# A two-layer attention and expert kernel: the up stage in another order, the attention's last rows in banks of their own, part of the routing on ScalarE

## The chip, the cores and the metric

One core of a Trainium2 chip runs the whole program. The time is that of the device for one execution, in microseconds (us). Before the change the median of three executions is 611.51 us.

## What is computed

The reference runs two layers over `x` (16 positions x 128 rows of 256 features, float32), each an attention and a feed-forward part with a layer norm ahead and a residual sum behind. The parts that the change touches are the first layer's quantized feed-forward part, the second layer's attention, and its routed experts.

```python
x = act_qdq(x)                                   # scale from max|x|, rounded to 16-bit steps
up = act_qdq(x @ lpbq_dequant(w_up).T)           # 256 -> 768
gate = act_qdq(x @ lpbq_dequant(w_gate).T)
gate = act_qdq(gate * fixed_qdq_u16(sigmoid(gate)))
o = act_qdq(gate * up); return o @ lpbq_dequant(w_down).T
...
scores = einsum('bhqd,bhkd->bhqk', q, k) / sqrt(16)      # 16 heads of 16, 16 batches of 128
out = einsum('bhqk,bhkd->bhqd', softmax(scores), v) @ w_o.T + b_o
...
logits = layernorm(x) @ w_router                          # 2048 tokens, 8 experts, top 2
pos = cumsum(mask_kt, axis=1) * mask_kt - 1.0             # place in the expert, capacity 160
y = combine(gate, relu(dispatch(x) @ wi) @ wo)            # expert width 1024
```

## The kernel before

Each engine has its own hand-written queue of instructions; semaphores (`s[...]`) order them against each other. There is no scheduler, so the order in the code of an engine is the order on the chip. The 16 batches are called rows here, numbered 0 to 15 (`NB` = 16). PSUM is cut into eight banks `ps[0]` to `ps[7]`; the names `pA`, `pB`, `pC` in a profile are banks 0 to 3, 4 and 5, 6 and 7.

The **up stage** begins when the gate product has been computed for all tokens and its overall maximum is known. TensorE makes 24 pieces of the up product (`product`, 128 x 512 each, bank `ps[2 + f]`). ScalarE moves each out of PSUM (`evacuate`, L632) and VectorE takes its maximum (`piece_max`, L1066). Beside that, 16 gate pieces of 128 x 768 go through five steps: to integers (`g_to_int`, on ScalarE at L646 for even pieces, on VectorE at L1091 for odd ones), sigmoid (L659, ScalarE), rounding (L664, ScalarE), product (`gate_sig`, L1095, VectorE) and maximum (`gs_max`, L1099, VectorE). The buffers `GI`, `SG` and `SI` of these steps hold two pieces each. The queues are loops over four chunks. At the end `whole_max(2, 2)` gathers the two maxima, and nothing of the next stage starts before them.

The **second attention** walks the rows with a lag: at step t, scores of row t+1, turned probabilities of row t and t-1 (`turn_0` to `turn_3`, L1652, copied out by `pt_copy`, L746), values of row t-1 (L1661), and the output of rows t-2 and t-3 (`o_turn` L1714, `attn_out` L1242, `a_turn` L1725, `a_out` L1731, `add_attn` L1228). All rows share banks 6 and 7 for turned probabilities and for `o_turn`, bank 5 for values and bank 4 for the output.

Behind the last row a layer norm (`norm4`, L868, in pairs of rows) feeds `d_turn` (L1743, copied out by `xt4`, L754) and the router's logits: rows 0 to 7 in one group (`d_logits`, L1751), rows 8 to 15 one by one (`d_row`, L1770). VectorE then finds the two best experts (one-hots in `OH`, L1322), the places, and which token fills which place of expert 0 (`select`, L1348, 16 compares of 128 x 192 in bf16). POOL reads the chosen rows with three indirect transfers (`rows_in`, L508), TensorE turns them (`e_turn`, L1868) and the first expert's products start (L1884). `keep_busy` (L1399) are TensorE products that nothing reads.

## Time and profile before

| | |
|---|---|
| median of 3 executions | 611.51 us (611.19 to 614.05) |
| the profiled execution | 611.87 us, of which its span is 610.1 us |
| TensorE matmul busy | 519.4 us (85% of the span) |
| VectorE busy | 387.2 us (63%) |
| ScalarE busy | 306.2 us (50%) |
| POOL busy | 152.6 us (25%) |

A row of the timeline gives the start, the time, the engine, the line of the kernel, the operation, output<-input, and in brackets how long the engine had been idle before it and who released it. The distance between two starts on one engine can be shorter than the duration, since an instruction without a wait starts before the one ahead has ended.

### The profile page before, as it was taken

How to read it: one execution, taken by the hardware profiler on the slowest of the kernel's cores; microseconds unless marked ns; L12 is line 12 of the kernel's file. 1: busy time of each engine (PE TensorE's matmuls, PEld its weight loads, DVE VectorE, ACT ScalarE, POOL GpSimd, SP SyncE). 2: the span in 40 equal slices, each digit the busy share in tenths (PEclk: the TensorE clock that was granted, in tenths of full speed). 3: DMA queues.
4: the chain of work that ended last, by engine and by line, in shares of the span. 5: the costliest groups of instructions: out<-in, count | busy, mean ns of one | idle time of the engine just before them, and what ended most of it. 6: DMA issues, size and time to landing. Idle time of an engine off the chain costs nothing.

```text
span 610.1 us, 9357 instructions
## 1 busy us (share of the span) xinstructions
PE 519.4 (85%) x3284; PEld 366.7 (60%) x3284; DVE 387.2 (63%) x944; ACT 306.2 (50%) x577; POOL 152.6 (25%) x218
## 2 busy tenths in 40 slices
PE   0859999799989900799989999986699999999994
PEld 0638866654434400687757677775566776777673
DVE  5666689845469989888699799986423332133101
ACT  1526658823389969781287788874022122211220
POOL 2715525000000000000323133111224445434431
PEclk9979999989989965899999999999599999999998
DMA  7900000000000000016000001015114445453410
GB/s 216 309 4 2 1 2 1 2 0 1 0 0 0 1 0 1 1 65 211 0 1 3 19 18 37 2 36 173 26 51 161 148 161 178 135 179 125 130 44 21
DMA packets 31994, 37.57 MB, mean 62 GB/s; under 512 B 8657, under 2 KB 27729, under 8 KB 31953
## 3 DMA queue, kind: packets, MB, share of 16 engines
q1 hardware_dynamic: 28880, 29.07, 14.6%
q0 software_dynamic: 3072, 7.95, 4.5%
q8 instruction: 26, 0.43, 0.3%
q14 instruction: 16, 0.12, 0.1%
HBM read 30.14 MB, written 6.88 MB: 61 GB/s over the span
## 4 chain that ended last, share of the span: by engine, by line
PE 58%; DVE 21%; ACT 11%; issue 6%; SPq 1%; DMA 1%; POOLq 0%; DVEq 0%; POOL 0%; ACTq 0%
PE pA L1884 11%; PE pB L1902 9%; PE pC L1614 6%; DVE rm L1248 5%; PE pA L1646 3%; DVE arena L1257 3%; PE pA L1576 3%; ACT arena L595 2%; PE pC L1488 2%; PE pC L1576 2%; PE pB L1576 2%; ACT XIT L684 2%; PE pC L1895 2%; ACT XIT L679 2%; DVE am L1066 1%
## 5 line engine op out<-in xcount | busy, mean ns | idle before, releaser
L474 POOL TENSOR_TENSOR arena<-KT,par 128x256 f32<-128x256 f32 x32 | 18.9, 612 | 254.2 <-DVE XIT L1171 191.5
L1884 PE MATMUL pA<-arena 128*128 128x320 f32 x256 | 74.1, 438 | 0.9 <-ACT arena L817 0.9
L824 ACT ACTIVATE arena<-pA 128x320 f32<-128x320 f32 x64 | 28.0, 437 | 71.9 <-PE pA L1884 71.2
L1902 PE MATMUL pB<-arena 128*128 128x256 f32 x256 | 59.3, 385 | 0.0
L1884 PEld LDWEIGHTS pA<-arena 128*128 128x128 f32 x256 | 47.4, 190 | 19.4 <-issue 1.1
L1902 PEld LDWEIGHTS pB<-arena 128*128 128x128 f32 x256 | 47.4, 190 | 9.4 <-issue 3.1
L1066 DVE TENSOR_REDUCE am<-arena 128x1 f32<-128x512 f32 (+1 forms) x48 | 32.0, 681 | 23.9 <-ACT arena L632 23.9
L1614 PE MATMUL pC<-wdnT,XIT 128*128 128x256 f32 x192 | 42.9, 381 | 1.8 <-DVE XIT L1171 1.8
L1614 PEld LDWEIGHTS pC<-wdnT,XIT 128*128 128x128 f32 x192 | 36.0, 190 | 7.9 <-DVE XIT L1171 2.8
L1652 PE MATMUL pC<-ident,arena 128*128 128x128 f32 x256 | 37.8, 280 | 2.7 <-DVE arena L1242 1.2
L1248 DVE TENSOR_REDUCE rm<-pA 128x16 f32<-128x2048 f32 x16 | 36.7, 2291 | 2.8 <-PE pA L1646 2.0
L1257 DVE TENSOR_TENSOR arena<-pA,rm 128x1024 f32<-128x1024 f32 x32 | 37.7, 1220 | 0.5
L746 ACT ACTIVATE arena<-pC 128x512 f32<-128x512 f32 x64 | 36.5, 594 | 2.4 <-PE pC L1652 2.2
L817 ACT ACTIVATE arena<-pA 128x320 f32<-128x320 f32 x16 | 6.1, 435 | 62.4 <-PE pA L1868 62.4
L510 POOL DMA_INDIRECT out<-arena,token x24 | 23.5, 978 | 54.8 <-DVE arena L1379 44.9
L508 POOL DMA_INDIRECT arena<-token_rows,token x24 | 24.2, 1010 | 46.8 <-DVE token L1358 27.0
L1652 PEld LDWEIGHTS pC<-ident,arena 128*128 128x128 f32 x256 | 27.9, 141 | 12.1 <-issue 8.3
L1364 DVE COPY gcol<-arena 128x3 f32<-128x3 f32 x8 | 1.4, 181 | 53.1 <-DMA arena<-token_rows,token 53.1
L735 ACT ACTIVATE arena<-arena 128x1024 f32<-128x1024 f32 x32 | 33.6, 1052 | 1.7 <-DVE arena L1257 0.7
L1399 PE MATMUL pB<-ident 128*128 128x128 f32 x66 | 12.1, 362 | 21.6 <-DVE arena L1144 21.6
L508 POOL DMA_INDIRECT arena<-out,token x24 | 23.7, 988 | 9.3 <-issue 7.0
L1399 PEld LDWEIGHTS pB<-ident 128*128 128x128 f32 x66 | 11.4, 271 | 21.7 <-issue 21.6
(316 smaller groups left out, 1134.4 us busy)
## 6 DMA issues: line engine op xcount, KB each, us to landing
arena<-in_L_ffn_wi SPq DMA_DIRECT2D x8, 1024.0 KB, 5.4
arena<-in_L_ffn_wo SPq DMA_DIRECT2D x8, 1024.0 KB
X<-in_x SPq DMA_DIRECT2D x4, 512.0 KB, 6.1
arena<-in_ctx SPq DMA_DIRECT2D x4, 512.0 KB, 5.7
out<-X SPq DMA_DIRECT2D x4, 512.0 KB, 3.0
token_rows<-arena SPq DMA_DIRECT2D x4, 512.0 KB, 5.6
arena<-in_L_ffn_w_up SPq DMA_DIRECT2D x1, 768.0 KB, 8.9
arena<-in_L_ffn_w_gate SPq DMA_DIRECT2D x1, 768.0 KB, 10.3
```

Source lines behind the costliest of these rows:

```text
L508: return nc.gpsimd.indirect_dma_start(out=sbuf[0:n, c, :], out_offset=None, in_=dram, in_offset=where, bounds_check=NB * S - 1, oob_is_err ...
L735: nc.scalar.activation(part, part, ACT.Exp).then_inc(s["p_ready"], 1)
L746: nc.scalar.activation(PT[:, u, 4 * g:4 * g + 4, :], pC[:, BANK_OF[g], :].rearrange("p (k n) -> p k n", k=4), ACT.Copy).then_inc(s["pt_rea ...
L824: nc.scalar.activation(HT[:, u, f, :], ps[2 + f % 2][:, 0:ROWS], ACT.Relu).then_inc(s["h_relu"], 1)
L1066: V_.tensor_reduce(am[:, 0 if name == "gate" else 1, cols(c * FT + f, 1)], t[:, f, cols(c, 512)], AX.X, ALU.max, apply_absolute_value=True ...
L1248: V_.tensor_reduce(rm[:, u, :], sco, AX.X, ALU.max).then_inc(s["rm_ready"], 1)
L1257: V_.tensor_tensor(PR[:, u, part], sco[:, part], rm[:, u, part].unsqueeze(2).broadcast_to([P, NH1 // 2, P]), ALU.subtract).then_inc(s["s_s ...
L1576: last = mm(ps[2 + f][:, :], w[:, k, f * P:(f + 1) * P], XITv[:, k, cols(c, 512)], start=(k == 0), stop=(k == KD - 1))
L1614: last = mm(ps[6 + u][:, 0:D], OT[:, u, f, :], wdnT[:, f, :], start=(f == 0), stop=(f == FT - 1))
L1652: last = tr(pC[:, BANK_OF[g], n * P:(n + 1) * P], PR[:, u, 4 * g + n, :], ident[:, :])
L1884: last = mm(ps[2 + f % 2][:, 0:ROWS], WI[:, u, k, f * P:(f + 1) * P], XET[:, u, k, :], start=(k == 0), stop=(k == KD - 1))
L1902: last = mm(ps[4 + c][:, 0:D], HT[:, u, f, c * P:(c + 1) * P], WO[:, u, f, :], start=(f == 0), stop=(f == NFT - 1))
```

## The change

Six edits are made together.

1. Up stage. The loops are written out. `GI` holds four pieces instead of two, and `SI` moves into the tensor `wgtT`. VectorE turns pieces 0, 1, 2, 4, 5, 8, 11 and 12 into integers (`GATE_DVE`), ScalarE the other eight. ScalarE moves up pieces 0 and 1 out ahead of the wait for the gate's scale; TensorE makes up piece 0 and half of piece 1 around the two small products of `whole_max(1, 1)`.
2. End of the second attention. Row 15's probabilities are turned into banks 0 to 3, its values go to bank 0 and its `o_turn` to bank 6; the outputs of rows 14 and 15 go to banks 3 and 5. The end of the walk is written out in a new order on three engines. The norm of rows 8 and 9 is made ahead of row 14's output, and that of rows 4 to 7 moves from VectorE to ScalarE (`norm4_act`).
3. Logits of rows 8 to 11 are made in one group of eight narrow products (`d_logits4`) and turned back (`d_back4`), in place of eight products of 8 columns.
4. The one-hots are written with the 8 rows of a group innermost, which is their order in memory. Before, the expert was innermost, at a step of 32 bytes in the output.
5. Expert 0's compares for rows 12 to 15 (`SEL_DVE` = 12) go to ScalarE, as Abs and then Relu, two instructions a row.
6. Expert 0's three transfers have a semaphore each. Each is turned when it lands, with 13, 4 and 2 `keep_busy` products ahead instead of 20, and ScalarE copies the result in two instructions, the first ahead of the last transfer's part.

Some semaphores are folded into others. The prefetch of expert weights waits for `u_again` in place of `g2_again`, one ScalarE instruction later.

```diff
+        GATE_DVE = (0, 1, 2, 4, 5, 8, 11, 12)
...
+        SEL_DVE = 12
         BANK_OF = (1, 1, 0, 0)
+        OUT_BANK = [4] * (NB - 2) + [3, 5]
...
-            g_to_int(0, 0)
-            up_chunk(0)
-            with act.Fori(1, 3) as c:
-                up_chunk(c)
-            up_chunk(3)
+            def g_to_int(b):
+                if b >= 4:
+                    act.wait_ge(s["gs_done"], b - 3)
+                nc.scalar.activation(GI[:, b % 4], F_b(G, b), ACT.Copy, scale=sc[:, 7:8]).then_inc(s["g_int_act"], 1)
+            def sigmoid(b):
+                mine = sum(r in GATE_DVE for r in range(b + 1))
+                if b in GATE_DVE:
+                    act.wait_ge(s["g_int_dve"], mine)
+                else:
+                    act.wait_ge(s["g_int_act"], b + 1 - mine)
+                if b >= 2:
+                    act.wait_ge(s["sig_int"], b - 1)
+                nc.scalar.activation(SG[:, b % 2], GI[:, b % 4], ACT.Sigmoid, scale=sc[:, 5:6]).then_inc(s["sig"], 1)
+            def sig_round(b):
+                act.wait_ge(s["sig"], b + 1)
+                if b >= 2:
+                    act.wait_ge(s["gs_done"], b - 1)
+                nc.scalar.activation(SI[:, b % 2], SG[:, b % 2], ACT.Copy, scale=65536.0).then_inc(s["sig_int"], 1)
+            def up_evacuate(lo, hi):
+                for n in range(lo, min(hi, 4 * FT)):
+                    evacuate(U, "up", n // FT, n % FT)
+            up_evacuate(0, 2)
+            for b in range(NB):
+                n = 2 + 3 * (b // 2) + b % 2
+                if b == 0:
+                    act.wait_ge(s["sc_gate"], 1)
+                sigmoid(b)
+                up_evacuate(n, n + 1)
+                sig_round(b)
+                if b % 2:
+                    up_evacuate(n + 1, n + 2)
+                if b + 2 < NB and b + 2 not in GATE_DVE:
+                    g_to_int(b + 2)
...
+            def g_to_int(b):
+                if b >= 4:
+                    dve.wait_ge(s["gs_done"], b - 3)
+                V_.tensor_scalar(GI[:, b % 4], F_b(G, b), sc[:, 7:8], None, ALU.mult).then_inc(s["g_int_dve"], 1)
+            def gate_sig(b):
                 dve.wait_ge(s["sig_int"], b + 1)
-                V_.tensor_tensor(F_b(G, b), GI[:, u], SI[:, u], ALU.mult).then_inc(s["gs_done"], 1)
+                V_.tensor_tensor(F_b(G, b), GI[:, b % 4], SI[:, b % 2], ALU.mult).then_inc(s["gs_done"], 1)
...
-            up_chunk(0)
-            with dve.Fori(1, 4) as c:
-                up_chunk(c)
+                V_.tensor_reduce(am[:, 0, cols(b, 1)], F_b(G, b), AX.XY, ALU.max, apply_absolute_value=True).then_inc(s["up_max"], 1)
+            def up_max(lo, hi):
+                for n in range(lo, min(hi, 4 * FT)):
+                    piece_max(U, "up", n // FT, n % FT)
+            g_to_int(0)
+            g_to_int(1)
+            up_max(0, 3)
+            g_to_int(2)
+            for b in range(NB):
+                n = 3 + 3 * (b // 2) + b % 2
+                gate_sig(b)
+                if b >= 1:
+                    gs_max(b - 1)
+                up_max(n, n + 1 + b % 2)
+                if b + 3 < NB and b + 3 in GATE_DVE:
+                    g_to_int(b + 3)
             gs_max(NB - 1)
...
+            u = (NB - 1) % 2
+            rsqrt(6, 12)
+            pt_copy(NB - 1, u, 0)
+            pt_copy(NB - 1, u, 1)
+            pt_copy(NB - 1, u, 2)
+            pt_copy(NB - 1, u, 3)
+            os_copy(NB - 2, 1 - u)
+            at_copy(NB - 3, u)
+            os_copy(NB - 1, u)
+            act.wait_ge(s["xr_ready"], 1)
+            norm4_act(4)
+            norm4_act(5)
+            at_copy(NB - 2, 1 - u)
+            at_copy(NB - 1, u)
+            norm4_act(6)
+            norm4_act(7)
+            xt4(0)
+            xt4(1)
...
+                if t == NB - 1:
+                    dve.wait_ge(s["row_stats"], 2 * NB + 12)
+                    variances(12, D)
                 if 0 <= t - 3 < NB:
                     add_attn(t - 3)
                 if 0 <= t - 2 < NB:
                     attn_out(t - 2, t % 2)
+            u = (NB - 1) % 2
+            stats4(NB - 4)
+            inverse_roots(6, 12)
+            V_.scalar_tensor_tensor(out=s2[:, 0:12], in0=mean[:, 0:12], scalar=-1.0, in1=rstd[:, 0:12], op0=ALU.mult, op1=ALU.mult)
+            norm4(0)
+            norm4(1)
+            norm4(4)
+            attn_out(NB - 2, 1 - u)
+            add_attn(NB - 3)
+            attn_out(NB - 1, u)
+            stats4(NB - 3)
+            norm4(5)
+            add_attn(NB - 2)
+            stats4(NB - 2)
+            add_attn(NB - 1)
+            stats4(NB - 1)
             dve.wait_ge(s["row_stats"], 3 * NB)
             variances(4, D, None, 12)
...
+            dve.wait_ge(s["d_bk"], 2)
+            link(V_.tensor_copy(LW[:, 8:12, :], ps[7][:, P:2 * P].rearrange("p (r e) -> p r e", r=4)[:, :, 0:NE]))
+            dve.wait_ge(s["d_row"], 4)
+            link(V_.tensor_copy(LW[:, 12:16, :], ps[6][:, 0:4 * NE].rearrange("p (b e) -> p b e", b=4)))
...
-                first = V_.tensor_tensor(OH[:, k], by_row(q1[:, :, :]), by_row(per_e(r1[:, :])), ALU.is_equal)
+                first = V_.tensor_tensor(OH[:, k].rearrange("p g t e -> p g e t"), by_row(q1[:, :, :]).rearrange("p g t e -> p g e t"),
+                                         by_row(per_e(r1[:, :])).rearrange("p g t e -> p g e t"), ALU.is_equal)
...
+            def select_act(b):
+                far = XCT[:, 1, 1:4, :].rearrange("p k n -> p (k n)").bitcast(BF16).rearrange("p (b c) -> p b c", b=NB - SEL_DVE)[:, b - SEL_DVE]
+                link(nc.scalar.activation(far, cidx[:, b // TG, :], ACT.Abs, scale=-1.0, bias=place[:, b // TG, 0, b % TG:b % TG + 1]))
+                nc.scalar.activation(SEL[:, 0, b, :], far, ACT.Relu, scale=-1.0, bias=1.0).then_inc(s["sel_act"], 1)
+            act.wait_ge(s["place_ready"], 1)
+            for b in range(SEL_DVE, NB):
...
             def e_turn(e, u, h):
                 if e == 0:
-                    keep_busy(ps[5], 20)
-                pe.wait_ge(s[f"xe_in{u}"], (h + 1) * 48)
+                    keep_busy(ps[5], 13)
+                    for c in range(3):
+                        pe.wait_ge(s[f"xe_first{c}" if c < 2 else "xe_in0"], 16)
+                        for k in range(KD):
+                            if c < 2:
+                                last = tr(ps[0][:, (2 * k + c) * P:(2 * k + c + 1) * P], XE[:, 0, c, k * P:(k + 1) * P], ident[:, :])
+                            else:
+                                last = tr(ps[4][:, k * SHORT:(k + 1) * SHORT], XE[0:SHORT, 0, c, k * P:(k + 1) * P], ident[0:SHORT, 0:SHORT])
+                        if c == 1:
+                            last.then_inc(s["xe_first_tr"], 1)
+                        if c == 2:
+                            last.then_inc(s["xe_tr"], 1)
+                        else:
+                            keep_busy(ps[5], 4 - 2 * c)
+                    return
+                pe.wait_ge(s[f"xe_in{u}"], (h + u) * 48 + (1 - u) * 16)
```

On VectorE at the start of the up stage, before: L1091 makes integers, L1095 the product, L1066 and L1099 the maxima of an up piece and of a product.

```order
L1091 TENSOR_SCALAR F<-arena,sc 128x768
L1095 TENSOR_TENSOR arena<-F 128x6x128
L1066 TENSOR_REDUCE am<-arena 128x1
L1095 TENSOR_TENSOR arena<-F 128x6x128
L1099 TENSOR_REDUCE am<-arena 128x1
L1066 TENSOR_REDUCE am<-arena 128x1
L1091 TENSOR_SCALAR F<-arena,sc 128x768
L1095 TENSOR_TENSOR arena<-F 128x6x128
L1099 TENSOR_REDUCE am<-arena 128x1
L1066 TENSOR_REDUCE am<-arena 128x1
L1095 TENSOR_TENSOR arena<-F 128x6x128
```

The same place of the changed kernel, where the same steps have the lines L1148, L1152, L1122 and L1156.

```order
L1148 TENSOR_SCALAR F<-arena,sc 128x768 x2
L1122 TENSOR_REDUCE am<-arena 128x1 x3
L1148 TENSOR_SCALAR F<-arena,sc 128x768
L1152 TENSOR_TENSOR arena<-F,wgtT 128x6x128
L1122 TENSOR_REDUCE am<-arena 128x1
L1152 TENSOR_TENSOR arena<-F,wgtT 128x6x128
L1156 TENSOR_REDUCE am<-arena 128x1
L1122 TENSOR_REDUCE am<-arena 128x1 x2
L1148 TENSOR_SCALAR F<-arena,sc 128x768
L1152 TENSOR_TENSOR arena<-F,wgtT 128x6x128
L1156 TENSOR_REDUCE am<-arena 128x1
```

Three integer pieces and three up maxima now stand ahead of the first product, where there were one and none.

On TensorE around row 15 of the second attention, before: L1652 turns probabilities, L1661 are values, L1731 is the output's product, L1714 turns values, L1725 turns the output, L1743 turns normed rows.

```order
L1661 MATMUL pB<-arena,V 32x128 x16
L1652 MATMUL pC<-ident,arena 128x128 x8
L1731 MATMUL pB<-wTo,arena 128x256 x2
L1714 MATMUL pC<-ident,arena 128x128 x4
L1652 MATMUL pC<-ident,arena 128x128 x4
L1725 MATMUL pB<-ident,arena 128x128 x2
L1661 MATMUL pB<-arena,V 32x128 x16
L1731 MATMUL pB<-wTo,arena 128x256 x2
L1714 MATMUL pC<-ident,arena 128x128 x4
L1743 MATMUL pA<-ident,arena 128x128 x4
L1725 MATMUL pB<-ident,arena 128x128 x2
L1743 MATMUL pA<-ident,arena 128x128 x4
```

The same place of the changed kernel, where those steps have the lines L1737, L1747, L1827, L1807, L1821 and L1842.

```order
L1737 MATMUL pA<-ident,arena 128x128 x8
L1747 MATMUL pB<-arena,V 32x128 x16
L1737 MATMUL pA<-ident,arena 128x128 x8
L1821 MATMUL pB<-ident,arena 128x128 x2
L1747 MATMUL pA<-arena,V 32x128 x16
L1807 MATMUL pC<-ident,arena 128x128 x4
L1827 MATMUL pB<-wTo,arena 128x256 x2
L1807 MATMUL pC<-ident,arena 128x128 x4
L1821 MATMUL pA<-ident,arena 128x128 x2
L1842 MATMUL pA<-ident,arena 128x128 x4
L1821 MATMUL pB<-ident,arena 128x128 x2
L1827 MATMUL pA<-wTo,arena 128x256 x2
```

Row 15's probabilities (L1737) are turned into `pA` in two groups of eight around row 14's values; its values go to `pA`, and the turns of rows 14 and 15 (L1807) stand closer together.

## Rows read from the trace of the kernel before

**Rows 1.** The page's chain of work that ended last: share of the span by engine.

```profile
...
PE 58%; DVE 21%; ACT 11%; issue 6%; SPq 1%; DMA 1%; POOLq 0%; DVEq 0%; POOL 0%; ACTq 0%
...
```

**Rows 2.** Stretch, then busy us (instructions) of PE, PEld, DVE, ACT, POOL; PEclk; DMA.

```profile
...
171.21:222.06 50.85, 42.03 (x95) 18.10 (x93) 46.74 (x66) 46.02 (x65) 0.00 (x0) 0.94 0.00 0
...
171.00:172.00 1.00, 1.00 (x2) 0.33 (x1) 0.78 (x4) 0.68 (x1) 0.00 (x0) 0.50 0.00 0
...
```

**Rows 3.** Timeline, VectorE's first product of the up stage (start us, us, what, idle before).

```profile
...
174.77 0.96 DVE L1095 TENSOR_TENSOR arena<-F 128x768 f32<-128x768 int16 x1 [2.95 <-ACT F L664]
...
```

**Rows 4.** Timeline of VectorE and ScalarE in the up stage's last chunk.

```profile
...
209.32 0.61 DVE L1091 TENSOR_SCALAR F<-arena,sc 128x768 int16 x1
...
209.84 0.95 DVE L1095 TENSOR_TENSOR arena<-F 128x768 int16 x1
209.96 0.94 ACT L659 ACTIVATE F<-F,sc 128x768 f32<-128x768 int16 x1 [0.64 <-DVE F L1091]
...
210.71 0.95 DVE L1099 TENSOR_REDUCE am<-arena  x1
210.81 0.58 ACT L632 ACTIVATE arena<-pA 128x512 f32<-128x512 f32 x1
...
211.28 0.83 ACT L664 ACTIVATE F<-F 128x768 uint16<-128x768 f32 x1
...
211.57 0.68 DVE L1066 TENSOR_REDUCE am<-arena  x1
...
212.02 0.92 ACT L646 ACTIVATE F<-arena,sc 128x768 int16<-128x768 f32 x1
...
```

**Rows 5.** Timeline from the attention's last row to the last logits.

```profile
...
403.41 1.05 ACT L735 ACTIVATE arena<-arena 128x1024 f32<-128x1024 f32 x1
...
404.12 0.63 PE L1652 MATMUL pC<-ident,arena 128*128 128x128 f32 x4 [1.24 <-DVE arena L1242]
...
406.62 1.09 ACT L746 ACTIVATE arena<-pC 128x512 f32<-128x512 f32 x2
...
412.41 0.42 DVE L1242 TENSOR_TENSOR arena<-pC,rs 128x256 f32<-128x256 f32 x1
...
413.81 1.13 PE L1731 MATMUL pB<-wTo,arena 128*128 128x256 f32 x4
...
418.05 1.38 DVE L868 TENSOR_SCALAR arena<-X,mean,rstd 128x256 f32<-128x256 f32 x4
...
418.19 1.95 PE L1770 MATMUL pB<-wrt,KT 128*128 128x8 f32 x16
...
423.38 0.19 DVE L1306 COPY XIT<-pC 128x32 f32<-128x32 f32 x1 [1.56 <-PE pC L1770]
...
```

**Rows 6.** Timeline of the routing: one-hots and the sixteen compares.

```profile
...
424.30 0.28 DVE L1319 TENSOR_TENSOR XIT<-XIT,r 128x128 f32<-128x128 f32 x1
424.42 0.31 ACT L811 ACTIVATE arena<-arena 128x128 f32<-128x128 f32 x1 [2.27 <-DVE arena L1314]
...
425.26 0.69 DVE L1322 TENSOR_TENSOR XIT<-XIT,r 128x128 bf16<-128x128 f32 x1
425.99 0.44 DVE L1327 SCALAR_TENSOR_TENSOR XIT<-XIT 128x64 f32<-128x64 bf16 x2
...
430.67 0.45 DVE L1348 TENSOR_SCALAR arena<-cidx,XIT 128x192 bf16<-128x192 bf16 x2
```

**Rows 7.** Timeline from the routed rows' reads to the first expert product.

```profile
...
435.20 7.13 PE L1399 MATMUL pB<-ident 128*128 128x128 f32 x40
...
439.42 0.97 POOL L508 DMA_INDIRECT arena<-token_rows,token  x1 [0.30 <-issue]
442.03 0.17 DVE L1364 COPY gcol<-arena 128x3 f32<-128x3 f32 x1 [6.50 <-DMA arena<-token_rows,token]
...
444.18 1.08 PE L1884 MATMUL pA<-arena 128*128 128x320 f32 x3 [0.86 <-ACT arena L817]
```

**Rows 8.** The same columns as rows 2, one us within the stretch of rows 7.

```profile
...
440.00:441.00 1.00, 1.00 (x10) 1.00 (x9) 0.00 (x0) 0.00 (x0) 0.39 (x1) 0.87 0.25 93
...
```

276 lines of the change are left out of this document (142 added, 134 removed).

## Prediction

> **What bounds the kernel now.** I read the chain that ended last first, then the timeline around each edit, then busy time by stretch. The chain is 58% TensorE, 21% VectorE and 11% ScalarE [rows 1]; no engine bounds the whole. In the up stage the chain leaves TensorE. From the gate's scale to the last maximum, 171.21 to 222.06, pass 50.85 us, with VectorE busy for 46.74, ScalarE for 46.02 and TensorE for 42.03 [rows 2]. VectorE and ScalarE hand pieces to and fro, and what either waits for is lost to both. The largest such wait is the first: VectorE idles 2.95 us before its first product at 174.77, since one gate piece has to pass sigmoid, evacuation and rounding [rows 3]. At the end of the attention the chain goes from engine to engine: TensorE waits 1.24 us to turn row 15's probabilities, until VectorE has read bank 7 (L1242) at 404.12, and row 15's own output is divided at 412.41 [rows 5]. From there to the first expert product at 444.18 nearly each instruction waits for the one before it, so that what is cut there counts in full.
>
> **1. Up stage.** I add up VectorE's queue by distances between starts, which the last chunk shows [rows 4]: an integer piece 0.52 (209.32 to 209.84), a product 0.87, a gate maximum 0.86, an up maximum 0.60. The change keeps the counts, 8, 16, 16 and 24: 4.16 + 13.92 + 13.76 + 14.40 = 46.24 us. So 50.85 holds 4.6 us of waits. ScalarE likewise: sigmoid 0.85, evacuation 0.47, rounding 0.74, and 0.92 less an overlap of 0.09 for an integer piece [rows 4], with counts 16, 24, 16, 8: 43.4 us, two of the evacuations now ahead of the scale. VectorE's queue is the longer.
>
> Does it run without waits? At the start VectorE has two integer pieces, three maxima and one more piece to do: 2 x 0.52 + 3 x 0.60 + 0.52 = 3.4 us. ScalarE meanwhile waits 0.6 for the first integers and needs 0.85 + 0.47 + 0.83 = 2.2, so the rounding is there at 2.8. Two pieces then cost VectorE 2 x 0.87 + 2 x 0.86 + 3 x 0.60 + 0.52 = 5.8 us and ScalarE 2 x 0.85 + 3 x 0.47 + 2 x 0.74 + 0.83 = 5.4. Going piece by piece through both queues, I find one wait of VectorE, 0.3 us for up piece 5; ScalarE is ahead by 0.03 us at piece 1 and by 0.4 to 2.0 from piece 2 on. Against it stands the scale itself: TensorE puts up pieces around the two small products of the maximum and makes them later by 0.2 together. The stage then ends at 171.21 + 0.2 + 46.24 + 0.3 + 0.1 = 218.05 in place of 222.06: **4.0 us**. TensorE's 42 us [rows 2] begin as soon as the last gate product is made, without waiting for the maximum, and stay covered. Bounds: 4.4 without that wait; below, 1.6 if each of ScalarE's instructions costs 0.05 more than I count (second case).
>
> **2. Attention's end.** Row 15's first turn goes into banks 0 to 3 and no longer waits the 1.24 [rows 5]. What is late next is ScalarE. Its second half of row 15's exponentials ends at 403.41 + 1.05 = 404.46. Behind it stand a root (two short instructions, an estimated 0.45), four copies at 0.50 (two take 1.09 for a single 0.59), another 0.50 and row 13's output copy, about 0.35: 407.8. Then TensorE's output product, 1.13 as it stands at 413.81 and an estimated 0.9 to the next start, row 15's turn with 0.63 as at 404.12 and a short reciprocal (0.3) give 409.7 for the division that was at 412.41 [rows 5]: 2.7 earlier. From there the old kernel needs 5.64 to the last normed rows at 418.05. The new one needs more, since ScalarE's queue now holds four norms ahead of `xt4(0)`. The trace has no such instruction of 256 elements; between 0.31 for 128 and 0.83 for 768 without a column operand, and 0.94 with one [rows 4, 6], I estimate 0.5 to 0.6 each. Two lie in ScalarE's idle time, and two push the copies; I take 0.6 back. So the last norm starts 2.1 earlier, at 415.95.
>
> **3. Logits.** Now TensorE spends 1.95 us on rows 8 to 11 from 418.19 [rows 5], and only then turns rows 12 and 13, whose norm began at 418.05. Eight narrow products of 128 columns take their place, an estimated 0.5 us, and they are done before that norm is. The remaining chain of 5.33 us, 418.05 to 423.38 [rows 5], becomes 4.2: **3.2 us with part 2**. Bounds: 3.8 if the norms are hidden; 1.2 if only part 3 works.
>
> **4. One-hots.** Two of them on the chain, 0.69 each at L1322, against 0.28 for the same 128 x 128 with both sides in order (L1319) [rows 6]. Now the output is in order and the input is read at a step of 32 bytes. L1327 reads its bf16 input at such a step and takes 0.44 for two with 64 elements each [rows 6]; if reads cost what the writes do, 0.41 / 128 per element, each would be 0.2 longer and there would be no room for that. I take 0.37: 2 x 0.32 = **0.6 us**; bounds 0 and 0.8. The Trainium skill (SBUF — State Buffer, "Door 1: The DMA port swizzle") says that accesses go by lines of 16 bytes and each new line costs, which makes no difference between reading and writing; by it the reading side would now pay and this part would give 0.
>
> **5. Compares on ScalarE.** VectorE's sixteen take 2.96 from 430.67, twelve of them 2.2 [rows 6]. ScalarE needs eight instructions of 192 elements, each second one waiting for the one before: 0.46 (with a column operand) + 0.28, so 4 x 0.74 + 0.1 = 3.05 by the same two points as in part 2. It ends last, 0.1 after the old time, but TensorE then has one product left instead of eight. I count **0**; bounds minus 0.4 and plus 0.5.
>
> **6. First turn.** Twenty `keep_busy` fill 435.20 to 442.3, the last transfer is seen at 442.03, and the expert starts at 444.18 [rows 7]. Thirteen take about 5.3, since the clock rises at about 440.2 [rows 8]: to 440.5. The transfers are issued 1.3 apart (the third at 439.42) [rows 7], so the first two have landed by 439.4 and 440.7. Turn 0.2, four fillers 0.9, turn 0.2, two fillers 0.4, and the last turn follows at 442.3, done at 442.65. ScalarE's small copy takes 0.4: 443.05, **1.1 us** earlier. Bounds 0.4 (fillers at the low clock) and 1.3.
>
> Folded semaphores cost nothing: VectorE and ScalarE do the same waits under other names. The prefetch of weights starts one ScalarE instruction later, long before the first expert needs them. The writes of rows to DRAM start earlier with the norms and stay behind part 2's work. The quantized products, the down stage and the experts are not touched and begin earlier as a whole.
>
> **Sum.** 4.0 + 3.2 + 0.6 + 0 + 1.1 = 8.9 us. The profiled execution took 611.87, so 603.0; it stands 0.36 above the median of 611.51, so I predict **602.6**.
>
> **The rivals**, at the median.
> - *ScalarE holds VectorE up in the up stage.* For it: ScalarE was busy 46.02 against my 43.4 [rows 2], and is ahead by only 0.03 at piece 1. At 0.05 more for each of 64 instructions my walk ends 2.4 later: 605.0. Chance 0.14.
> - *TensorE's clock falls at the start of that stage again.* In 171 to 172 it is granted 0.50, the 1.2 GHz level, [rows 2]; ahead of that it had stood mostly idle while the gate's maximum was found. Now it works through, so it should stay at 2.4 GHz. If it doesn't, up pieces 2 and 3 come 3.4 later and the stage gives 0.6: 606.0. Chance 0.06.
> - *The separate banks don't free the last rows*, because ScalarE's queue is full anyway. Then parts 2 and 3 give 1.2: 604.6. Chance 0.10.
> - *Reads at a step cost what writes do.* 603.2. Chance 0.07. The Trainium skill's page named in part 4 would have it so.
> - *Slower.* The fillers are cut and split, and the clock comes back not at 440.2 [rows 8] but late in the first expert. Each us at the low level costs half of one. Against 8.9 of gain it decides from 18 us on, and for slower by over 0.5% needs 24 us: then 614.6 or more. Against it: the fillers ahead of 440.2 are the same products in the same place, and behind it the gaps between turns are filled. Chance 0.03.
>
> **How the numbers follow.** The forecast has 0.60, with a range of its own of 601.2 to 604.4 from the bounds of parts 1, 4, 5 and 6 (not all on one side). The range reaches down to 600.9, past which only all upper bounds together lead (600.6), and up to 606.4, which holds the first four rivals and leaves out the slower one and sums of two. One measurement of this kernel tells about 0.5%, 3.1 us, from no change. All cases but the last are faster by more; two rivals with all lower bounds give 2.8 to 3 us, hence 0.04 for the same: 0.93, 0.04, 0.03.
>
> **What would show it.** Right: from the gate's scale to the last maximum 46.7 us, VectorE's first product with little idle ahead, TensorE at full clock in 171 to 172; row 15's division near 405.8 on the new clock (4.0 less); 10.4 us from it to the last logits' copy (11.0 before); L1389 at 0.37; 7.9 us from the routed places' fillers to the first expert product in place of 9.0. Wrong: VectorE waiting for L674 in the steady part, ScalarE's norms on the chain, or products of 0.2 us and more per 128 columns behind the turn.

## The result, and the profile after

The changed kernel took 602.25 us (median of 4; the kernel before beside it 611.35, median of 4). The ratio is 0.983, with a 95% interval of 0.980 to 0.986: faster by 1.5 to 2.0%. Five later executions had a median of 601.66 against 611.58, a ratio of 0.984 (0.983 to 0.986). The forecast was 602.6, with 601.2 to 604.4 as its own range. The ratio times 611.51 is 601.0, which lies 0.2 below that range, though inside the wider one of 600.9 to 606.4; the median of the four as it stands, 602.25, lies inside both. The profiled execution took 602.22, of which 600.5 are its span. One execution of a later run (655.83 us, granted clock 0.824) and one of the kernel before beside it (661.42, 0.819) were slow as a whole and are in no ratio.

The page's chain of work that ended last, to be read against [rows 1]. ScalarE's share fell from 11% to 9%, and that of `issue`, time in which an engine waited for nothing that the profile shows, from 6% to 4%:

```profile
PE 59%; DVE 23%; ACT 9%; issue 4%; SPq 1%; DMA 1%; POOLq 0%; POOL 0%; DVEq 0%
```

The up stage by stretch, columns as in [rows 2], and VectorE's first product, which stands in [rows 3] for the kernel before:

```profile
169.60:216.64 47.04, 37.76 (x88) 16.36 (x87) 46.53 (x67) 44.60 (x64) 0.00 (x0) 0.96 0.00 0
171.00:172.00 1.00, 1.00 (x3) 0.38 (x2) 0.95 (x3) 0.89 (x3) 0.00 (x0) 1.00 0.00 0
```
```profile
170.66 2.01 DVE L1122 TENSOR_REDUCE am<-arena 128x1 f32<-128x512 f32 x3
172.58 0.61 DVE L1148 TENSOR_SCALAR F<-arena,sc 128x768 int16<-128x768 f32 x1
173.11 0.95 DVE L1152 TENSOR_TENSOR arena<-F,wgtT 128x768 f32<-128x768 int16 x1
```

VectorE has three maxima and a third integer piece to do while ScalarE makes the first sigmoid, and goes from them to its product without a gap. It is busy for 46.53 of the 47.04 us. The wait of 2.95 us is gone, and so is most of the 4.6 that lay in the stage.

The attention's end, with row 15's maximum as the point from which both kernels are counted (398.34 before, 392.87 after, 5.47 apart). First that row of the kernel before, then the changed kernel:

```profile
398.34 2.29 DVE L1248 TENSOR_REDUCE rm<-pA 128x16 f32<-128x2048 f32 x1
```
```profile
392.87 2.29 DVE L1305 TENSOR_REDUCE rm<-pA 128x16 f32<-128x2048 f32 x1
...
404.21 0.42 DVE L1299 TENSOR_TENSOR arena<-pC,rs 128x256 f32<-128x256 f32 x1
...
410.49 1.38 DVE L926 TENSOR_SCALAR arena<-X,mean,rstd 128x256 f32<-128x256 f32 x4
...
412.51 0.60 PE L1842 MATMUL pA<-ident,arena 128*128 128x128 f32 x4
...
412.94 1.91 PE L1881 MATMUL pC<-wrt,KT 128*128 128x8 f32 x16
...
414.96 0.19 DVE L1372 COPY XIT<-pC 128x32 f32<-128x32 f32 x1 [1.65 <-PE pC L1881]
```

Against [rows 5], less the 5.47, the division comes 2.73 earlier, the last norm 2.09 and the last logits' copy 2.95. Row 15's division and the last norm are where the prediction put them. The narrow products of the last four rows (L1881) still stand in one block of 1.91 behind the last turn, as they did before (1.93 from 421.35).

The one-hots, the compares and the first expert, against [rows 6, 7]:

```profile
418.86 0.38 DVE L1389 TENSOR_TENSOR XIT<-XIT,r 128x128 bf16<-128x128 f32 x1
...
421.13 0.29 DVE L1410 TENSOR_TENSOR XIT<-XIT 128x128 f32<-128x128 f32 x1
...
421.46 2.24 DVE L1417 TENSOR_SCALAR arena<-cidx,XIT 128x192 bf16<-128x192 bf16 x12
...
423.69 0.44 ACT L858 ACTIVATE F<-cidx,XIT 128x192 bf16<-128x192 bf16 x1
...
424.17 0.36 ACT L859 ACTIVATE arena<-F 128x192 bf16<-128x192 bf16 x1
...
424.96 0.56 DVE L1424 CAST XIT<-pC 128x384 bf16<-128x384 f32 x1 [1.26 <-PE pC L1976]
...
425.91 5.57 PE L1473 MATMUL pB<-ident 128*128 128x128 f32 x26
...
432.91 0.17 DVE L1438 COPY gcol<-arena 128x3 f32<-128x3 f32 x1 [6.68 <-DMA arena<-token_rows,token]
...
433.25 0.33 PE L1999 MATMUL pB<-ident,arena 64*128 64x64 f32 x2
433.62 0.28 ACT L870 ACTIVATE arena<-pB 128x128 f32<-128x128 f32 x1
433.95 0.57 PEld L2029 LDWEIGHTS pA<-arena 128*128 128x128 f32 x3 [0.50 <-ACT arena L870]
433.95 0.81 PE L2029 MATMUL pA<-arena 128*128 128x320 f32 x2 [0.37 <-ACT arena L870]
```

The place of the kernel before:

```profile
430.34 0.29 DVE L1342 TENSOR_TENSOR XIT<-XIT 128x128 f32<-128x128 f32 x1
```

A one-hot takes 0.38 for 0.69. From the last logits' copy to the place (`place`, 421.13 and 430.34) pass 6.17 for 6.96. From the fillers to the first expert product pass 8.04 for 8.98. The copy of the gate column (L1438, 432.91) marks the landing of the last routed rows.

These two profiles hold two things that the change doesn't explain. The first expert product comes 10.23 us earlier (444.18 and 433.95), but the spans differ by only 9.6; and 1.6 of the 10.23 were there when the product that makes the gate's scale started (170.83 and 169.22), ahead of any changed instruction but TensorE's first pieces.

### The profile page after: what moved, and what is told of

Same layout as the page of the kernel before. It is cut to its first block, busy times and chain, and to the rows that moved or that the text cites. A ratio compares the mean times of both kernels' runs of the same rounds, so it can differ in the third digit from the quotient of the medians.

```text
span 600.5 us, 9206 instructions
## 1 busy us (share of the span) xinstructions
PE 514.1 (86%) x3283; PEld 363.0 (60%) x3283; DVE 384.6 (64%) x937; ACT 310.0 (52%) x590; POOL 153.0 (25%) x218
## 4 chain that ended last, share of the span: by engine, by line
PE 59%; DVE 23%; ACT 9%; issue 4%; SPq 1%; DMA 1%; POOLq 0%; POOL 0%; DVEq 0%
PE pA L2029 12%; PE pB L2047 9%; PE pC L1699 6%; DVE rm L1305 5%; PE pA L1731 3%; DVE arena L1314 3%; ACT arena L607 3%; PE pA L1654 2%; PE pC L1562 2%; PE pB L1654 2%; PE pC L1654 2%; ACT XIT L704 2%; PE pC L2040 2%; DVE am L1156 2%; DVE arena L1152 2%
## 5 line engine op out<-in xcount | busy, mean ns | idle before, releaser
L1122 DVE TENSOR_REDUCE am<-arena 128x1 f32<-128x512 f32 x48 | 32.1, 681 | 23.0 <-ACT arena L644 22.9
L1737 PE MATMUL pC<-ident,arena 128*128 128x128 f32 x240 | 35.4, 280 | 1.5 <-ACT XIT L740 0.8
L1438 DVE COPY gcol<-arena 128x3 f32<-128x3 f32 x8 | 1.5, 182 | 53.3 <-DMA arena<-token_rows,token 44.4
L768 ACT ACTIVATE arena<-pC 128x512 f32<-128x512 f32 x60 | 34.2, 595 | 1.4 <-PE pC L1737 1.1
L1737 PEld LDWEIGHTS pC<-ident,arena 128*128 128x128 f32 x240 | 26.1, 141 | 10.5 <-issue 6.9
L1473 PEld LDWEIGHTS pB<-ident 128*128 128x128 f32 x64 | 11.4, 274 | 21.7 <-issue 21.6
```

The lines of the kernel that those rows point to most:

```text
L768: nc.scalar.activation(PT[:, u, 4 * g:4 * g + 4, :], bank.rearrange("p (k n) -> p k n", k=4), ACT.Copy).then_inc(s["pt_ready"], 1)
L1122: V_.tensor_reduce(am[:, 0 if name == "gate" else 1, cols(c * FT + f, 1)], t[:, f, cols(c, 512)], AX.X, ALU.max, apply_absolute_value=True ...
L1737: last = tr(bank[:, n * P:(n + 1) * P], PR[:, u, 4 * g + n, :], ident[:, :])
```

## The experiments

All stage times below run from the start of the scale's product (`sc[:, 7:8]`) to the start of the reduction of the up maxima (`gm[:, 1:2]`). By this measure the changed kernel's up stage is 169.22 to 216.72, 47.50 us, and that of the kernel before 51.35; for the changed kernel it is 0.46 more than the stretch of the fence above. The marks, before and then after:

```profile
170.83 0.21 DVE L1085 TENSOR_SCALAR sc<-sc 128x1 f32<-128x1 f32 x1
...
222.18 0.17 DVE L1118 TENSOR_REDUCE gm<-am 128x1 f32<-128x24 f32 x1
```
```profile
169.22 0.21 DVE L1141 TENSOR_SCALAR sc<-sc 128x1 f32<-128x1 f32 x1
...
216.72 0.17 DVE L1177 TENSOR_REDUCE gm<-am 128x1 f32<-128x24 f32 x1
```

The measure leaves out what the scale itself costs: it comes 3.70 behind the last gate evacuation with TensorE's pieces around the maximum, and 3.52 in the kernel before, so 0.18 goes off each gain.

**The changed kernel again.** No edit.

> The changed kernel once more, unaltered, to see what of its 10.23 us lead at the first expert's product was there before any changed instruction. In the first pair of traces the last evacuation of the gate stage already came 1.79 us earlier, 1.40 of it in 121 to 126 us, where TensorE was granted 0.50 in the kernel before and 1.00 in the changed one, in code that both have. Theory: that difference comes and goes from one execution to the next. Then this profile shows the last gate evacuation anywhere between 165.5 and 167.3, and the stages behind it as before: the up stage 47.0 from the scale to the row of maxima, and 232.6 from there to the last logits' copy less what is inside. Rival: it belongs to the changed program (where its code or its data lie), and then the gate stage ends at 165.5 again, within 0.1, and the clock is 1.00 at 122 to 125. Time 600 to 602.5 in either case.

601.66 us. The stage took 47.50 again, and the maxima stand 198.24 ahead of the last logits' copy in both profiles. The scale came at 168.64, 0.6 earlier than in the first profile, and the last gate evacuation at 164.94, below the band that I gave (165.5 to 167.3). The clock was 1.00 at 122 to 126 again, as the rival had it. So the start differs from one execution to the next, but this run alone doesn't settle theory against rival; the further profiles of the kernel before, below, do.

**The old up stage in the changed kernel.** ScalarE, VectorE and TensorE:

```diff
-            g_to_int(0)
-            g_to_int(1)
-            up_max(0, 3)
-            g_to_int(2)
...
+            up_chunk(0)
+            with dve.Fori(1, 4) as c:
+                up_chunk(c)
```

> The changed kernel with the up stage of the kernel before on all three engines (two tiles of integers, the whole maximum ahead of the first pieces, the old order), all else as changed. Theory of the prediction: the stage is 50.9 again from the scale to the row of maxima against 47.0, the scale comes 0.2 earlier, and everything behind it shifts by 3.7, so the first expert's product comes at 437.6 to 439.5 by the clock phase ahead, and the time is 605.5 to 607 against 602.25, a ratio to the kernel before of 0.990 to 0.993. Rival one, the clock phase gave much of the gain in this stage: the stage stays under 49. Rival two, the 1.79 ahead of the stage depends on the new stage: it is gone here and the time is over 607.5.

606.2 us (ratio 0.991, 0.989 to 0.992), and the stage 51.69. The new stage is worth 4.2 us, 4.0 less the later scale. The rival that gave it to the clock phase ahead falls (the stage isn't under 49), and so does the second one (the time isn't over 607.5). VectorE's first product:

```profile
173.03 0.96 DVE L1143 TENSOR_TENSOR arena<-F 128x768 f32<-128x768 int16 x1 [3.34 <-ACT F L676]
```

**TensorE alone as before.**

```diff
-            up_half(0, 0)
-            up_half(0, 1).then_inc(s["up_done"], 1)
-            max_turn(1, 1)
-            up_half(1, 0)
-            max_spread(1, 1)
-            up_half(1, 1).then_inc(s["up_done"], 1)
-            for n in range(2, 4 * FT):
+            whole_max(1, 1)
+            for n in range(4 * FT):
                 up_half(n, 0)
                 up_half(n, 1).then_inc(s["up_done"], 1)
```

> The changed kernel with one thing undone in the up stage: TensorE does the gate's whole maximum ahead of the first up pieces, as in the kernel before, instead of between them. Theory: TensorE then stands still while VectorE works out the maximum, the granted clock falls to 0.50 at the start of the stage (as it was in 171 to 172 of the kernel before), the first pieces take twice as long and VectorE waits for them, since its first up maxima now come ahead of its first gate product. The scale comes 0.2 earlier and the stage is 1.0 to 2.0 longer than 47.0, net 0.8 to 1.8 later at the row of maxima. Rival: the pieces are not what the engines wait for, and the stage is 47.0 within 0.3, so that TensorE's order was worth nothing or the loss of 0.2.

606.16 us (0.991, 0.989 to 0.993), stage 51.50. One engine's order of a few instructions gives back the whole gain of the stage. My 1.0 to 2.0 was far too small, and the rival's nothing further off. By stretch, then the three engines in the timeline:

```profile
168.00:169.00 1.00, 1.00 (x2) 0.48 (x3) 0.86 (x7) 0.00 (x0) 0.00 (x0) 0.50 0.00 0
169.00:170.00 1.00, 1.00 (x3) 0.48 (x2) 1.00 (x3) 0.00 (x0) 0.00 (x0) 0.50 0.00 0
```
```profile
166.42 0.27 PE L1634 MATMUL pA<-ident,gm 128*1 128x128 f32 x1 [1.62 <-DVE gm L1135]
...
167.30 0.58 PE L1638 MATMUL pA<-gd,ones 1*128 1x1 f32 x2 [0.61 <-DVE gd L1091]
...
167.81 5.13 PE L1675 MATMUL pA<-XIT,wupT 128*128 128x512 f32 x8
...
171.26 0.60 ACT L644 ACTIVATE arena<-pA 128x512 f32<-128x512 f32 x1 [4.53 <-PE pA L1675]
171.89 0.69 DVE L1122 TENSOR_REDUCE am<-arena 128x1 f32<-128x512 f32 x1 [1.81 <-ACT arena L644]
```

In the new order ScalarE puts two evacuations, and VectorE three up maxima, ahead of the first sigmoid's product. If the pieces are late, both engines stand behind them in their own queues.

**The same two, with fillers in TensorE's wait.** The question is how much of this is the clock. Both runs have the maximum ahead of the pieces, with products that nothing reads ahead of and behind its first small product: one with the new order of VectorE and ScalarE, one with the old.

```diff
+            keep_busy(ps[1], 6)
             max_turn(1, 1)
+            keep_busy(ps[1], 2)
             max_spread(1, 1)
```

> The run before last (the gate's whole maximum ahead of the first pieces, all else as changed) with fillers put into TensorE's wait: six ahead of the turn of the column of maxima, two between the turn and the spreading product. The same order, but the engine doesn't stand still. That run lost 3.9 in the stage: the first piece took from 167.81 to 171.2 at a granted 0.50, ScalarE waited 4.53 for it and VectorE 4.2 in all for ScalarE. Theory: nearly all of that is the clock, so with 1.00 granted the first piece is there 1.1 behind the spreading product, and the row of maxima comes 0.3 to 1.2 later than in the changed kernel counted from the last gate evacuation (which was 51.2 there), against 4.0 later without fillers. Rival: it is the order, the pieces begin after the maximum at whatever clock, and the loss stays above 2.5.

> The changed kernel with the whole up stage as in the kernel before, and the same eight fillers in TensorE's wait. Without fillers the clock was 0.50 in 168 to 171 and the stage 51.7 from the scale to the row of maxima, VectorE waiting 3.34 for the first integer sigmoid and ScalarE only 0.57 for the first piece. Theory: in the old order ScalarE's own chain of three 0.9 activations holds VectorE, so the clock is worth little here: the stage comes to 51.0 to 51.5. Rival: the clock was what cost 4 in the kernel before, and the stage with the old order falls to under 49, so that the new order itself was worth little.

The granted clock was 1.00 from 165 to 179 in both. With the new order the stage took 50.07 (ratio 0.988, 0.985 to 0.990), with the old one 50.99 (603.71 us, 0.988, 0.986 to 0.989). The waits that remain:

```profile
169.81 3.70 PE L1675 MATMUL pA<-XIT,wupT 128*128 128x512 f32 x8
...
171.83 0.60 ACT L644 ACTIVATE arena<-pA 128x512 f32<-128x512 f32 x1 [2.89 <-PE pA L1675]
```
```profile
171.12 0.96 DVE L1143 TENSOR_TENSOR arena<-F 128x768 f32<-128x768 int16 x1 [2.66 <-ACT F L676]
```

With the new order the loss against 47.50 is 2.57 at full clock and 4.00 without fillers: the clock is 1.43 of it. The expectation counted from the last gate evacuation to the maxima, which takes the scale in: 51.20 in the changed kernel, 55.22 without fillers, 53.59 with them. By that count the loss is 2.39, twice the theory's upper end of 1.2 and just under the rival's 2.5. Neither had the size right; the order is the larger part and the clock the smaller. With the old order the theory holds (50.99 for 51.0 to 51.5): the clock is worth 0.70.

**TensorE new, the other two old.**

> The changed kernel with VectorE's and ScalarE's up stage as in the kernel before, but TensorE's new order (first pieces around the gate's maximum). The fifth run has the new order of VectorE and ScalarE with the pieces late, at a full clock: 50.1 from the scale to the row of maxima; the sixth has the old order with them late at a full clock: 51.0. Theory: the gain needs both halves. ScalarE does its own integers and sigmoid ahead of the first piece in the old order, so pieces that lie ready earlier win nothing: the stage is 50.7 to 51.2, and 0.2 of scale is lost. Rival: TensorE's early pieces carry the gain by themselves, and the stage is 48.5 or less.

605.05 us (0.988, 0.986 to 0.990), stage 51.00 at a clock of 1.00. Against the 50.99 of the old order with fillers, early pieces win nothing when ScalarE doesn't take them first, and the scale comes 0.18 later. The stage in one table:

| VectorE and ScalarE | TensorE's first pieces | clock at the start | stage, us |
|---|---|---|---|
| old | behind the maximum | 0.50 | 51.69 (kernel before, four profiles: 51.35 to 51.66) |
| old | behind, fillers | 1.00 | 50.99 |
| old | around it | 1.00 | 51.00 |
| new | behind | 0.50 | 51.50 |
| new | behind, fillers | 1.00 | 50.07 |
| new | around it | 1.00 | 47.50 |

**The one-hots as before.** The output in `OH`'s order again, `by_row(...)` without the turned view.

> The changed kernel with the two one-hots written as in the kernel before (output running along each place's token rows with a step, input in order), all else as changed. Theory of the prediction: each takes 0.69 again instead of 0.38, so the first selection's compares start 0.62 later behind the last logits' copy: 7.12 instead of 6.50. Rival: the saving belongs to something else than the order of writing (the compares around it) and the interval changes by less than 0.2. The whole time can't show it: it should lie within 0.3% of the changed kernel's.

Each took 0.69, and the place came 6.79 behind the last logits' copy for 6.17: 0.62, as forecast.

**One bank for the last outputs.**

```diff
-        OUT_BANK = [4] * (NB - 2) + [3, 5]
+        OUT_BANK = [4] * NB
...
+            a_out(NB - 2, 1 - u)
+            d_turn(1)
             a_turn(NB - 1, u)
-            a_out(NB - 2, 1 - u)
             a_out(NB - 1, u)
-            d_turn(1)
```

With the bank goes TensorE's order: row 15's turn has to stand behind row 14's output product and wait for row 14's sum. The run measures both together.

> The changed kernel with one thing undone in the attention's end: the last two rows' outputs go through the same bank as all others, so row 15's turn waits for row 14's sum, and stands behind row 14's output product in TensorE's order. Theory: row 15's turn moves from 404.7 to about 406.2, its sum from 406.9 to about 408.5, ScalarE's last two norms and its copies behind them as much, and the last logits' copy comes 1.2 to 1.8 later behind row 15's division (10.75 in the changed kernel). Rival: the turn is hidden behind the norms and copies of the other rows, and the interval grows by less than 0.5.

From row 15's division to the last logits' copy pass 12.24 us (404.11 to 416.35) for 10.75: 1.49 more, within the theory's band. VectorE's sum of row 15 shows the wait:

```profile
408.58 0.42 DVE L1286 TENSOR_TENSOR X<-pB,X 128x256 f32<-128x256 f32 x1 [1.74 <-PE pB L1827]
```

**All compares on VectorE** (`SEL_DVE = 16`), and **the first turn as before** (`keep_busy(ps[5], 20)`, one wait, six turns).

> The changed kernel with all sixteen compares of the first selection on VectorE. In the changed kernel's trace the first twelve take 2.24 on VectorE and end at 423.70, the four pairs on ScalarE end at 424.53, 3.07 after their start. Theory of the prediction: handing over four was worth nothing. Sixteen take 2.98, and the cast of the tokens starts 3.40 to 3.50 behind the start of the compares, as in the changed kernel (3.50). Rival: sixteen small instructions need more than their own time, and the cast comes over 0.3 later than there.

> The changed kernel with the first expert's turn as in the kernel before: twenty fillers, one wait for all three gathers, six turns in a row, two copies of 0.39 each. Theory of the prediction: the first expert's product comes 9.0 behind the start of the fillers, against 8.04 in the changed kernel. Rival: the rows land together and the turns are hidden anyway, and it is 8.3 or less. The next expert's turn waited for its own rows in both profiles (0.74 in the kernel before, 1.30 in the changed one); if this wait takes up part of the loss again, the whole time moves less than 0.9.

```profile
422.97 2.96 DVE L1417 TENSOR_SCALAR arena<-cidx,XIT 128x192 bf16<-128x192 bf16 x16
...
426.54 0.56 DVE L1424 CAST XIT<-pC 128x384 bf16<-128x384 f32 x1 [0.62 <-PE pC L1976]
```
```profile
426.09 7.08 PE L1461 MATMUL pB<-ident 128*128 128x128 f32 x40
...
435.09 1.07 PE L2002 MATMUL pA<-arena 128*128 128x320 f32 x3 [0.85 <-ACT arena L868]
```

The cast comes 3.57 behind the start for 3.50: handing four compares over is worth 0.07. The first turn took 9.00 for 8.04, a loss of 0.96. This stretch repeats less well than the others: it took 7.53 to 8.22 in the twelve profiles with thirteen fillers, 8.87 to 8.98 in the four of the kernel before. The loss is clear, its size is between 0.8 and 1.5.

**Thirteen compares on VectorE and ten fillers**, meant to be better than the changed kernel.

```diff
-        SEL_DVE = 12
+        SEL_DVE = 13
-                    keep_busy(ps[5], 13)
+                    keep_busy(ps[5], 10)
```

> Meant to be better than both: the changed kernel with thirteen compares on VectorE and three on ScalarE (ScalarE's four ended 0.83 behind VectorE's twelve), and ten fillers instead of thirteen ahead of the first expert's first turn, since the last turn started 0.34 behind the landing of its rows. Theory: the cast comes 0.5 to 0.65 earlier behind the start of the compares (2.85 to 3.0 against 3.50), the first expert's product 0.3 earlier behind the fillers (7.7 against 8.04), together 0.8 to 1.0, a time of about 601.2 against 602.1, too little to show in the times beside what differs from one execution to the next. Rival one: fewer fillers let the clock fall to 0.50 at the first turns, and the second interval is 8.5 or more. Rival two: the second expert's rows, whose transfers queue behind the first's, take all of it back, and its turn waits 0.8 longer.

```profile
424.04 0.56 DVE L1424 CAST XIT<-pC 128x384 bf16<-128x384 f32 x1 [0.62 <-PE pC L1976]
...
431.92 0.34 PE L1999 MATMUL pB<-ident,arena 64*128 64x64 f32 x2
431.99 0.17 DVE L1438 COPY gcol<-arena 128x3 f32<-128x3 f32 x1 [6.66 <-DMA arena<-token_rows,token]
```

600.44 us (598.91 to 600.86), 0.979 of the kernel before (0.977 to 0.982). The cast comes 3.04 behind the start (0.46 less), the first expert product 7.62 behind the fillers (425.00 to 432.62, 0.42 less). Together 0.88, as in the theory. The 0.46 is shown: the cast comes 3.50 behind in each of the twelve profiles with twelve compares. The 0.42 is one profile against one: the changed kernel's second profile has 7.91, and with thirteen fillers 7.53 occurred too. What can be seen is that the last turn no longer stands behind the landing of its rows (431.92 and 431.99, for 433.25 and 432.91). In the times its interval lies below that of the changed kernel's five executions (0.983 to 0.986) and touches that of its first four; the two were not run beside each other.

**Where the rest lies: three more profiles of the kernel before, and the end of the stage moved** by four and by six repeats of its last maximum.

> The kernel before once more, unaltered, for the stretch ahead of the change: its first profile had TensorE at 0.50 from 123 to 126 and the gate's scale at 170.83, all five profiles of the changed kernel and its variants have 1.00 there and the scale between 168.56 and 169.22. Theory: the clock differs between executions of the same code, and a second look at the kernel before shows 1.00 in 122 to 126 with the scale at 168.5 to 169.5. Rival: the changed kernel starts that stretch in another phase of its own, and the kernel before shows 0.50 there again with the scale at 170.5 or later.

> The kernel before, a third profile: the gate's scale comes between 167.5 and 171, the clock rises 3 to 4 behind the fillers' start where that is at 245 or later and 9 or more behind it where it is at 243.4 to 244.5, if the theory of the place holds. If chance decides, the rise doesn't go with the place.

> The kernel before, a fourth profile, as the third: between the four, the scale's time and the place of the fillers tell how much of the difference between the first two profiles was there ahead of any changed instruction.

> The changed kernel with the last gate product's maximum worked out four times more, one after the other, ahead of the row of maxima: 4.1 to 4.3 of VectorE's time that moves everything behind it later, so that the fillers ahead of the down products start at about 243.7 instead of 239.6. Theory: whether the clock rises in time depends on when in the execution the fillers come, so the rise is now 9 or more behind their start and the time grows by 5.2 to 5.4, to about 607.4. Rival: the late rise belongs to the old up stage (how TensorE's work is spread in it) or is chance; then the rise is 2.9 to 3.7 behind the start again and the time is about 606.2.

> The same with six repeats, 6.2 to 6.4: the fillers start at about 245.8, where the first profile of the kernel before has them (245.55, clock in time). Theory: the clock rises 2.9 to 3.7 behind their start, and the time is 6.3 over the changed kernel's, about 608.3, only 0.9 over the run with four repeats though 2.1 of work lies between them. Rival: the rise doesn't depend on the place, and the two runs differ by 2.1, or the rise is late here as well.

The scale came at 168.53, 168.92 and 169.32 in the three, after 170.83 in the first. The nine profiles with the whole changed up stage have it at 168.56 to 170.75. So what the first pair showed ahead of the change is no gain of the change. A stretch of unchanged code within 120 to 127 has its part in it; two executions of the kernel before, by stretch:

```profile
122.00:126.00 4.00, 3.93 (x19) 3.83 (x20) 1.79 (x5) 0.00 (x0) 0.00 (x0) 0.60 0.00 0
```
```profile
122.00:126.00 4.00, 4.00 (x20) 2.58 (x19) 1.42 (x2) 0.47 (x1) 0.00 (x0) 1.00 0.00 0
```

Between the same two instructions of ScalarE around it (119.09 and 127.83 in the first profile) pass 8.74 us with the clock at 0.50 there and 7.34 without. It fell in two of the four profiles of the kernel before and in two of the seven with nothing changed back in the up stage and nothing added to it, so it favours neither kernel.

A second such place are the fillers ahead of the down products. The third and the fourth profile of the kernel before, TensorE by timeline:

```profile
243.65 3.33 PE L1399 MATMUL pB<-ident 128*128 128x128 f32 x14 [21.57 <-DVE arena L1144]
...
248.58 1.61 PE L1399 MATMUL pB<-ident 128*128 128x128 f32 x12
```
```profile
244.25 3.32 PE L1399 MATMUL pB<-ident 128*128 128x128 f32 x14 [21.57 <-DVE arena L1144]
...
249.51 2.93 PE L1399 MATMUL pB<-ident 128*128 128x128 f32 x12
```

In one the second fillers run at 2.4 GHz, in the other at 1.2 GHz, and there the clock rises 9.5 behind the first filler, when the down products have begun; what follows up to the last logits' copy then takes 1.0 to 2.1 longer. That happened in two of four profiles of the kernel before (1.1 each), in three of the five with an up stage wholly or partly undone, and in none of the seven with the changed one in its place. The place doesn't decide it: with four repeats the fillers start at 244.37 and the clock rises in time (606.55 us), with six at 246.89 and it rises 11 behind. The theory of the place fell on both. The second's median of 608.32 came out as it said, but its profiled execution took 610.30 at a mean granted clock of 0.937, and the other four had 0.945 to 0.948. Whether the late rise belongs to the old up stage or to chance isn't shown: none in seven against five in nine is little to go by, and the one with six repeats was late with the new stage.

The 0.6 given back in the experts is a third. TensorE waits for the second expert's rows, 0.35 to 1.32 us, and its first turn of them stands 149.8 us ahead of the end in each of the eighteen profiles, so what lies behind that turn is the same in all. In the changed kernel it waited 1.30 in the first profile and 0.59 in the second.

## Where the prediction held and where it failed, step by step

- **What failed: unchanged code, put at nothing.** The sum says that the quantized products, the down stage and the experts "are not touched and begin earlier as a whole", and has no term for them. Its parts, each between two marks, gave less than forecast (8.4 for 8.9, below), and yet the time fell by more: 10.5 us by the first ratio, 9.7 by the second, 9.1 and 9.9 by the medians. So 0.7 to 2.1 us came from outside the parts. What the runs show there is TensorE's clock ahead of the down products, which rose late in two of four profiles of the kernel before, at 1.1 each, and in none of the seven with the changed stage. How often it does so in executions without a trace can only be guessed from their mean granted clock. Of 34 executions of the kernel before beside later runs, 27 have 0.939 to 0.944, like the two late profiles (0.943), with a median of 612.4; seven have 0.947, like the two in time, with 611.07. The nine of the changed kernel have 0.948 to 0.953. By this estimate the late clock makes 0.5 to 1 us of it. The rest stays open, and so does the reason why the clock rises late.
- **Up stage, 4.0.** Measured 3.81 in the first pair (50.85 to 47.04), less 0.18 for the later scale, so 3.63; 3.99 between the means of four profiles (51.49) and seven (47.50), by the other marks, less the same, so 3.81. The size held, but a step of the mechanism failed. That VectorE's queue of 46.2 sets the end, and that there is one wait, held: 0.38 where 0.3 was counted. What the prediction did not see is what its walk hangs on. It took the early pieces as cover (their 42 us "stay covered") and their price as 0.2, and gave only the clock as a way for them to fail. That rival's time, 606.0, was met by TensorE's old order (606.16), but by luck: the clock is 1.43 of its 4.00. The other 2.57 is that ScalarE's and VectorE's new orders ask for pieces 0 to 2 first, 1.72 us of TensorE each even at full clock.
- **Attention's end and logits, 3.2.** Division 2.73 earlier (2.7 forecast), last norm 2.09 (2.1), last copy 2.95 (3.2). The remaining chain is 4.47, not 4.2. Of its gain of 0.86, 0.84 lies between the last norm and the last turn (2.02 for 2.86); behind that turn nearly nothing changed, since the block of the last four rows' products is as long as before. ScalarE's norms took 0.59 to 0.63 each, with 0.49 from one start to the next (0.5 to 0.6 forecast). The own banks, with TensorE's order that they allow, carry 1.49. No run undoes the rest of parts 2 and 3 (row 15's turn into banks 0 to 3, the norms on ScalarE, the grouped logits); their shares are read from the traces.
- **One-hots, 0.6.** 0.62, each 0.38 (0.37 forecast). By the rule of the Trainium skill (SBUF — State Buffer, "Door 1: The DMA port swizzle") this part would have been 0, with reads at a step costing what writes do; the runs disagree: a read at 32 bytes adds 0.09 to 0.29, a bf16 write at the same step 0.40. Only the old and the new write order were run, not a read at the step by itself. A further 0.17 in this stretch (0.79 in all) is mostly a shorter way from the last copy to the next reduction (0.23 for 0.39), which I did not isolate.
- **Compares, 0.** 0.07.
- **First turn, 1.1.** 0.94 in the first pair, 0.96 undone. The last turn stood 0.34 behind its rows, since the fillers ran over; with ten that is gone.
- **Sum.** 3.6 + 2.95 + 0.8 + 0.1 + 0.95 = 8.4 for 8.9 forecast, of which the up stage misses 0.4 and the attention's end 0.25. Single executions of the changed kernel differ by more than the whole miss (599.73 to 603.06). In the range, all upper bounds together lead to 600.8, not 600.6.

The rivals fell: ScalarE doesn't hold VectorE (one wait of 0.38), the banks do free the rows, a read at a step costs less than a write, and the clock came back at 431.0, 5.1 behind the first filler as before (435.20 and 440.3), ahead of the first expert.

## What to carry to other kernels

When queues of several engines are reordered together, check each reordered piece against the others' old order: one engine's part, worth nothing by itself, can be the condition for all the rest. Price a late producer by what stands behind it in the queues of the engines that take its pieces, not by the producer's own delay. And compare stretches between two marks rather than spans: this stage repeated to 0.01 us in seven profiles, while whole executions differed by 3.

## What the runs showed of the hardware

- In unchanged code TensorE's granted clock differed between executions: 0.50 or 1.00 for 3 to 4 us within 120 to 127, and 2.9 to 3.7 or 9.2 to 11.4 us from the first filler to the rise ahead of the down products. The first costs 1.4 us and the second 1.0 to 2.1, and I found no place or gap that decides between them.
- In the six profiles in which TensorE stood still for 1.62 and 0.61 us around the gate's maximum, the clock fell to 0.50 within 0.9 us behind the second standstill and stayed there for 3 to 4 us. In the twelve with eight fillers in the wait, or with pieces around the maximum, it stayed at 1.00.
- On VectorE, a 128 x 128 instruction that writes bf16 at a step of 32 bytes took 0.69 us, one that reads float32 at that step 0.38, and one with both sides in order 0.28 to 0.29.
